# One VectorE operation per head for the joined rows of later node tiles, and tanh in place of Exp for their shares

## The chip, the cores and the metric

The kernel runs on one core of one Trainium2 chip. The metric is the time of one execution on the device in microseconds (us), the median of several runs; 1% of it, 40 us, is about what a measurement of this kernel can tell from no change.

## What is computed

A graph attention layer over 6250 nodes with 256 features (4 heads of 64) and 206250 directed edges, added to the input through a relu, and then 30 iterations of a small feed-forward step on every node, added as well:

```python
def _gat_forward(x, edge_index, W, att_src, att_dst, bias):
    h = (x @ W).reshape(n, HEADS, HID)
    a_src = jnp.einsum('nhf,hf->nh', h, att_src)
    a_dst = jnp.einsum('nhf,hf->nh', h, att_dst)
    # edges: the given ones and one from every node to itself
    e = jax.nn.leaky_relu(a_src[src] + a_dst[dst], NEG_SLOPE)
    m = jax.ops.segment_max(e, dst, num_segments=n)
    num = jnp.exp(e - m[dst])
    denom = jax.ops.segment_sum(num, dst, num_segments=n)
    alpha = num / denom[dst]
    out = jax.ops.segment_sum(alpha[:, :, None] * h[src], dst, num_segments=n)
    return jax.nn.relu(out.reshape(n, HEADS * HID) + bias)

def step(h, _):                       # 30 times
    h = h + 0.01 * jnp.tanh(h)
    h = h * jax.nn.sigmoid(h)
    h = _layernorm(h, ln_w, ln_b)
    h = jnp.einsum('bsc,dc->bsd', h, W) + b
    return (h, None)

x = x + gat(_layernorm(x))
x = x + scan(step, _layernorm(x), 30)
```

## The kernel before

The 6250 nodes lie in 49 tiles of 128 rows (`X[P, NT, C]`, node p*49+t). `attention` fills the first 2477 us: it walks the sorted edges in 124 steps and leaves in DRAM, for every node, one row of 264 numbers (`sums`): for each head 64 weighted feature sums and the sum of the weights, and behind them the four maxima the weights were taken against. The edge from a node to itself is left out there; the node's own row with its four exponents stands in `haug` and `eself`.

`scan_ffn` follows. It joins the two for every node and runs the 30 iterations. Joining takes, per tile and head: the gathered maximum and the own exponent (`nmax`), both less that maximum (`below`), their Exp on ScalarE (`share`, L1347), the denominator `den` from the gathered weight sum times one share plus the other share, and `part`, both shares over `den` (function `norms`). Then the gathered row `S` times `part[0]` plus the own row `own` times `part[1]`, a relu, and the sum with `X`.

The 49 tiles come in eight parts, `FT = [0, 4, 8, 14, 21, ...]`. The first three (`FRONT = 3`) are joined before the iterations start. The other five, seven tiles each, are joined while the iterations of earlier nodes run; `Plan` holds for each of these parts the pass at which each stage begins and the distance between its tiles. Part 3 takes a tile every 3 passes, parts 4 to 7 one every 11 passes, with 80 passes from one part to the next. The stages of a later tile before the change: `fetch` (GpSimd issues the indirect DMA that gathers the row into `S`), `scale` (VectorE writes `S` times `part[0]` into `Hs`, one TENSOR_TENSOR of 128x256, L1492), `own` (GpSimd multiplies the own rows in place, L1294), `add` (TensorE adds the two by products with the identity into the PSUM tile `ps_m`, L1652 and L1653), `both` (VectorE, relu and sum with X, reading `ps_m`, L1504), `spread` (statistics, L1507); behind the seventh tile come `mean`, `root` and, on ScalarE, `ready` (L1362), which writes the normalised rows into `Hs` and makes the tile's chunk available.

The iterations are 750 passes, each one iteration of one chunk of two tiles (25 chunks, the last with one tile), in an order that `passes` works out from the passes at which chunks become ready. A pass of chunk q is: tanh on ScalarE (`th`, L1409), the addition on GpSimd (`h1`, L1301), silu on ScalarE (`h2`, L1386), statistics and their aggregate on VectorE (L1568, L1577), the inverse root on GpSimd (L1308, for three passes at once from pass 54), the transposition, the product with W on TensorE (L1676), and on VectorE the scaling from PSUM with the bias (`affine`, L1586). The transposition is TensorE's (L1662, copied by ScalarE, L1392) for the first 54 passes and every third afterwards; the others go through DRAM: ScalarE splits the words (`hs`, L1398), one DMA stores them and a transposing DMA reads them back.

Each engine's program is written out pass by pass: a function `step` per engine says what it issues at pass n, with fixed offsets (VectorE's statistics are for pass n+3, its affine for n-2 from pass 54; TensorE's product for n-4), and `due` puts the stages of the later parts at the start of a step. ScalarE, GpSimd and VectorE take their instructions in that order, so a stage that waits holds all that is behind it.

## Time and profile before

| what | us |
|---|---|
| median of 3 runs | 4014.36 |
| lowest and highest | 4007.2, 4033.22 |
| the profiled execution | 4010.27 |
| its span in the trace | 4008.5 |
| busy: PE, DVE, ACT, POOL | 1551.2, 3057.0, 2421.6, 3000.3 |

PE is TensorE's products, PEld its weight loads (beside the products), DVE VectorE, ACT ScalarE, POOL GpSimd. Busy shares over the whole span say little here, as the attention part and the iterations have different limits; the argument goes by stretches. A timeline row gives the start, the duration, the engine, the line, the operation, its output and inputs and how many instructions it groups. Durations of neighbours overlap a little, so what an engine can do at most is read from start to start while it does not idle.

### The profile page before, as it was taken

The page shows a single profiled execution, that of the slowest core. Times are in us where ns is not written, and L with a number is a line of the kernel's source. Part 1 is how long each engine was busy: PE and PEld are TensorE (multiplying, and loading weights), DVE is VectorE, ACT ScalarE, POOL GpSimd, SP SyncE. Part 2 cuts the span into 40 slices and gives each one's busy share as a digit, 9 for nine tenths or more (in the row PEclk, how much of TensorE's full clock was granted, in tenths as well). Part 3 has the DMA queues.
Part 4 walks back from the last instruction along what each step waited for, and adds up shares of the span by engine and source line. Part 5 has one row for each costly group of instructions (what it writes and reads, how often), then busy time and mean ns, then how long its engine had stood idle before and what let it go on. Part 6 is the DMA issues. An engine that isn't in the chain of part 4 may idle for free.

```text
span 4008.5 us, 38964 instructions
## 1 busy us (share of the span) xinstructions
PE 1551.2 (39%) x7562; PEld 1329.0 (33%) x7562; DVE 3057.0 (76%) x7257; ACT 2421.6 (60%) x3681; POOL 3000.3 (75%) x2871
## 2 busy tenths in 40 slices
PE   3400000000000000000000001899999999999998
PEld 2300000000000000000000001788888888888887
DVE  7467585867768577685867766788988989888898
ACT  4334353534434344353534344689999999999997
POOL 7676676767676676766767672899999998889887
PEclk8755555555555555555555555999999999999999
DMA  7355565656555565565656563047777777777677
GB/s 201 113 177 193 182 207 181 213 174 214 195 190 201 169 223 178 190 209 168 225 164 218 189 198 126 23 117 179 189 185 185 181 177 177 173 177 175 177 183 193
DMA packets 649205, 720.45 MB, mean 180 GB/s; under 512 B 513249, under 2 KB 515458, under 8 KB 632948
## 3 DMA queue, kind: packets, MB, share of 16 engines
q1 hardware_dynamic: 563604, 486.62, 40.7%
q0 software_dynamic: 83824, 230.16, 20.0%
q10 hardware_dynamic: 1536, 1.18, 0.1%
q14 instruction: 178, 1.46, 0.1%
q8 instruction: 63, 1.03, 0.1%
HBM read 249.79 MB, written 352.38 MB: 150 GB/s over the span
## 4 chain that ended last, share of the span: by engine, by line
issue 25%; PE 20%; ACT 12%; DVE 12%; POOL 10%; DMA 9%; another core or an unknown queue 8%; SPq 2%; DVEq 0%; ACTq 0%; POOLq 0%
PE ps L1676 17%; ACT G L654 7%; POOL G L747 6%; DVE RS L983 5%; DMA turned<-hs 3%; DVE psum L964 3%; POOL h L1301 2%; PE ps L1662 2%; DMA h2T<-turned 2%; DMA sums<-G 2%; SPq L1231 1%; ACT hs L1398 1%; DMA G<-haug,idx 1%; ACT th L1409 1%
## 5 line engine op out<-in xcount | busy, mean ns | idle before, releaser
L747 POOL DMA_INDIRECT G<-haug,idx x1612 | 1526.6, 947 | 713.1 <-issue 481.8
L1676 PE MATMUL ps<-WT,h2T 128*128 128x256 f32 x5880 | 1338.8, 381 | 19.9 <-DMA h2T<-turned 18.8
L1676 PEld LDWEIGHTS ps<-WT,h2T 128*128 128x128 f32 x5880 | 1091.7, 191 | 175.8 <-DMA h2T<-turned 40.5
L983 DVE TENSOR_TENSOR_SCAN RS<-keep,psum 128x845 f32<-128x845 f32 x496 | 939.8, 1897 | 186.9 <-remote 109.9
L1301 POOL TENSOR_TENSOR h<-Hs,th 128x512 f32<-128x512 f32 (+1 forms) x750 | 937.8, 1262 | 129.9 <-ACT th L1409 124.6
L1068 PE MATMUL psum<-AD,ones 128*128 128x512 f32 x2 | 2.1, 1142 | 2284.9 <-DVE AD L1085 2284.9
L646 ACT ACTIVATE decay<-el,ZC 128x4 f32<-128x4 f32 x124 | 37.1, 299 | 1278.4 <-remote 568.0
L654 ACT ACTIVATE G<-RS 128x845 f32<-128x845 f32 x496 | 782.0, 1723 | 43.4 <-DVE RS L983 34.0
L1586 DVE SCALAR_TENSOR_TENSOR Hs<-ps,rs,b 128x256 f32<-128x256 f32 x1470 | 675.0, 459 | 145.3 <-PE ps L1676 132.6
L1068 PEld LDWEIGHTS psum<-AD,ones 128*128 128x128 f32 x2 | 0.5, 313 | 2285.2 <-DVE AD L1085 2285.2
L1568 DVE BATCH_NORM_STATS2 cst<-h 128x6 f32<-128x256 f32 x1470 | 546.3, 412 | 37.5 <-ACT h L1386 36.4
L964 DVE TENSOR_TENSOR psum<-G,psum 128x845 f32<-128x845 f32 x496 | 479.0, 1030 | 67.1 <-issue 62.9
L1386 ACT ACTIVATE h<-h 128x512 f32<-128x512 f32 (+1 forms) x750 | 459.4, 613 | 66.1 <-POOL h L1301 65.2
L1398 ACT ACTIVATE hs<-h 128x1024 uint16<-128x1024 uint16 x444 | 464.8, 1047 | 9.9 <-DMA turned<-hs 9.5
L1409 ACT ACTIVATE th<-Hs 128x512 f32<-128x512 f32 (+1 forms) x750 | 458.3, 611 | 7.5 <-DVE Hs L1586 6.7
L1308 POOL TENSOR_TENSOR rs<-cmv,half_neg 128x6 f32<-128x6 f32 (+1 forms) x286 | 353.1, 1235 | 14.7 <-DVE cmv L1577 13.7
L973 DVE SCALAR_TENSOR_TENSOR psum<-RS,decay,psum 128x65 f32<-128x65 f32 x492 | 125.3, 323 | 205.9 <-remote 205.6
L1662 PE MATMUL ps<-ident,h 128*128 128x128 f32 x1164 | 180.5, 277 | 24.5 <-ACT h L1386 18.1
L1577 DVE BATCH_NORM_AGGREGATE cmv<-cst 128x2 f32<-128x9 f32 x1470 | 188.1, 168 | 1.1
L1392 ACT ACTIVATE h2T<-ps 128x512 f32<-128x512 f32 (+1 forms) x306 | 171.4, 561 | 18.1 <-PE ps L1662 17.9
L1662 PEld LDWEIGHTS ps<-ident,h 128*128 128x128 f32 x1164 | 146.4, 142 | 61.7 <-ACT h L1386 26.0
L922 DVE TENSOR_TENSOR z<-G,AD 128x52 f32<-128x52 f32 x124 | 29.9, 241 | 165.8 <-DMA G<-haug,idx 132.3
(164 smaller groups left out, 1196.9 us busy)
## 6 DMA issues: line engine op xcount, KB each, us to landing
sums<-G SPq DMA_DIRECT2D x124, 1716.0 KB
turned<-hs SPq DMA_DIRECT2D x444, 256.0 KB
G<-haug,idx POOLq DMA_INDIRECT x1612
h2T<-turned SPq DMA_TRANSPOSE x444
haug<-G SPq DMA_DIRECT2D x7, 924.0 KB
X<-x SPq DMA_DIRECT2D x7, 784.0 KB
out<-X SPq DMA_DIRECT2D x24, 224.0 KB
own<-haug SPq DMA_DIRECT2D x5, 924.0 KB, 5.5
```

Of the source, the lines that this page charges most:

```text
L654: last = nc.scalar.activation(G[:, k % R, :, h * HR:(h + 1) * HR].rearrange("p t f -> p f t"), RS[:, k % 2, h, :, :], ACT.Copy)
L747: pool.indirect_dma_start(out=G[:, u, t, :], out_offset=None, in_=haug[:, :], in_offset=bass.IndirectOffsetOnAxis(ap=idx[:, i % 2, u * T + ...
L964: last = v.tensor_tensor(ps_m[:, h, :, :].rearrange("p f t -> p t f"), G[:, u, :, h * HR:(h + 1) * HR], w, ALU.mult)
L983: v.tensor_tensor_scan(RS[:, k % 2, h, :, :].rearrange("p f t -> p (f t)"), keep[:, k % 2, :, :].rearrange("p f t -> p (f t)"), ps_m[:, h, ...
L1301: g.tensor_tensor(h1[:, q.t, 0:n], chunk_rows(Hs, q.j, q.w), th[:, q.t, 0:n], ALU.add).then_inc(s_add, 1)
L1386: nc.scalar.activation(h2[:, q.u, 0:n], h1[:, q.t, 0:n], ACT.Silu, scale=1.0 / HS).then_inc(s_silu, 1)
L1398: nc.scalar.activation(hs[:, q.t, :].bitcast(U16).rearrange("p (l c) -> p l c", l=2), h2[:, q.u, :].bitcast(U16).rearrange("p (c l) -> p l ...
L1409: nc.scalar.activation(th[:, q.t, 0:n], chunk_rows(Hs, q.j, q.w), ACT.Tanh, scale=1.0 / HS).then_inc(s_tanh, 1)
L1568: last = v.bn_stats(cst[:, q.v, a, 0:6], h2[:, q.u, a * C:(a + 1) * C])
L1586: ins = v.scalar_tensor_tensor(out=Hs[:, q.j * CH + a, :], in0=ps_g[q.u][:, a * C:(a + 1) * C], scalar=rs[:, q.v, a:a + 1], in1=b100[:, :] ...
L1662: last = nc.tensor.transpose(ps_x[q.x][:, n * P:(n + 1) * P], h2[:, q.u, n * P:(n + 1) * P], ident[:, :])
L1676: last = nc.tensor.matmul(ps_g[q.u][:, a * C:(a + 1) * C], h2T[:, q.u, (a * 2 + k) * P:(a * 2 + k + 1) * P], WT[:, k, :], start=(k == 0), ...
```

## The change

For the later parts the gathered rows are no longer scaled into `Hs` ahead of time, and TensorE no longer adds. One VectorE operation per head (`joined`, 64 columns, four for a tile) takes `S` times `part[0]` plus the own rows, all in SBUF, into `Hs`, one step behind it the relu and the sum with `X` read `Hs` instead of PSUM. The two shares are written as 1 + tanh(d/2) and 1 - tanh(d/2) with d the difference of the two exponents, which have the same ratio as the two Exp; this holds for all eight parts. The maximum goes, an addition of 1.0 comes. Ahead of the first part a tanh of one column is issued on ScalarE. The plans lose a stage, and mean, root and ready come 4 passes earlier (3 for part 3), with which the order of the passes shifts in places. The semaphore of an own-row load is now one per buffer. The diff, cut where lines only rename:

```diff
-    def __init__(self, fetch, pace, below, share, norm, scale, own, add, both, step, mean, root, ready, every):
+    def __init__(self, fetch, pace, below, share, norm, own, join, both, step, mean, root, ready, every):
         n = QT
         self.at = dict(fetch=(fetch, pace, n), below=(below, 1, 1), share=(share, 1, 1), norm=(norm, 1, 1),
-                       scale=(scale, step, n), own=(own, step, n), add=(add, step, n), both=(both, step, n),
+                       own=(own, step, n), join=(join, step, n), both=(both, step, n),
...
-PLANS = {FRONT: Plan(5, 1, 10, 17, 15, 16, 22, 23, 21, 3, 43, 48, 50, 1)}
+PLANS = {FRONT: Plan(5, 1, 10, 17, 15, 20, 18, 19, 3, 40, 45, 47, 1)}
 for b in range(FRONT + 1, NF):
     q = 24 + 80 * (b - FRONT - 1)
-    PLANS[b] = Plan(q, 8, q + 54, q + 62, q + 63, q + 64, q + 70, q + 72, q + 72, 11, q + 141, q + 148, q + 151, 3)
+    PLANS[b] = Plan(q, 8, q + 54, q + 62, q + 63, q + 69, q + 67, q + 68, 11, q + 137, q + 144, q + 147, 3)
...
-        nmax = sb("nmax", [P, 2, QT, H])
-        below = sb("below", [P, 2, 2, QT, H])
+        apart = sb("apart", [P, 2, 2, QT, H])
         share = sb("share", [P, 2, 2, QT, H])
+        spare = sb("spare", [P, 1])
...
-            loads = {PLANS[b - 2].last("add") + 2: b for b in range(FRONT + 2, NF)}
+            loads = {PLANS[b - 2].last("own") + 2: b for b in range(FRONT + 2, NF)}
...
-                    pool.wait_ge(s_weighted, tiles_before(b - 1))
+                    pool.wait_ge(s_joined, tiles_before(b - 1))
...
-                nc.scalar.activation(share[:, b % 2, :, 0:n, :], below[:, b % 2, :, 0:n, :], ACT.Exp).then_inc(s_share, 1)
+                nc.scalar.activation(share[:, b % 2, :, 0:n, :], apart[:, b % 2, :, 0:n, :], ACT.Tanh, scale=0.5).then_inc(s_share, 1)
...
+            act.wait_ge(s_merged, 16)
+            nc.scalar.activation(spare[:, :], half_neg[:, 0:1], ACT.Tanh)
...
-                ch.add(v.tensor_tensor(nmax[:, i, 0:n, :], S[:, i, 0:n, SUMS:ROW], eself[:, t0:t1, :], ALU.max))
-                ch.wait()
-                v.tensor_tensor(below[:, i, 0, 0:n, :], S[:, i, 0:n, SUMS:ROW], nmax[:, i, 0:n, :], ALU.subtract)
-                v.tensor_tensor(below[:, i, 1, 0:n, :], eself[:, t0:t1, :], nmax[:, i, 0:n, :], ALU.subtract).then_inc(s_below, 1)
+                v.tensor_tensor(apart[:, i, 0, 0:n, :], S[:, i, 0:n, SUMS:ROW], eself[:, t0:t1, :], ALU.subtract)
+                v.tensor_tensor(apart[:, i, 1, 0:n, :], eself[:, t0:t1, :], S[:, i, 0:n, SUMS:ROW], ALU.subtract).then_inc(s_below, 1)
...
+                ch.add(v.tensor_scalar(share[:, i, :, 0:n, :], share[:, i, :, 0:n, :], 1.0, None, ALU.add))
+                ch.wait()
...
+            def joined(b, i):
+                for h in range(H):
+                    c = slice(h * HR, h * HR + HID)
+                    last = v.scalar_tensor_tensor(out=Hs[:, FT[b] + i, h * HID:(h + 1) * HID], in0=S[:, b % 2, i, c],
+                                                  scalar=part[:, b % 2, 0, i, h:h + 1], in1=own[:, b % 2, i, c],
+                                                  op0=ALU.mult, op1=ALU.add)
+                return last
...
-                if due(q, "scale"):
-                    b, i = due(q, "scale")
+                if due(q, "both"):
+                    b, i = due(q, "both")
+                    dve.wait_ge(s_joined, tiles_before(b) + i + 1)
+                    added(b, i, i + 1, Hs[:, FT[b] + i, :]).then_inc(s_taken, 1)
+                if due(q, "join"):
+                    b, i = due(q, "join")
                     if i == 0:
                         dve.wait_ge(s_part, b + 1)
-                    gathered(b, i, i + 1).then_inc(s_weighted, 1)
-                if due(q, "both"):
-                    b, i = due(q, "both")
-                    n = tiles_before(b) + i
-                    dve.wait_ge(s_joined, n + 1)
-                    added(b, i, i + 1, ps_m).then_inc(s_taken, 1)
+                    dve.wait_ge(s_ownt, tiles_before(b) + i + 1)
+                    joined(b, i).then_inc(s_joined, 1)
...
-            def add_tile(b, i):
-                n = tiles_before(b) + i
-                pe.wait_ge(s_weighted, n + 1)
-                pe.wait_ge(s_ownt, n + 1)
-                wait_count(pe, s_taken, n)
-                to = heads(ps_m, HID)
-                nc.tensor.matmul(to, ident[:, :], heads(Hs[:, FT[b] + i, :], HID), start=True, stop=False)
-                nc.tensor.matmul(to, ident[:, :], heads(own[:, b % 2, i, :], HR), start=False, stop=True).then_inc(s_joined, 1)
...
-                if due(p, "add"):
-                    add_tile(*due(p, "add"))
```

In the order of instructions of VectorE, at the third tile of part 3 (`S` the gathered rows, `partw` the shares over the denominator, `ps` PSUM, `X` the residual), before:

```order
L1586 SCALAR_TENSOR_TENSOR Hs<-ps,rs,b 128x256
L1568 BN_STATS cst<-h 128x6 x2
L1586 SCALAR_TENSOR_TENSOR Hs<-ps,rs,b 128x256
L1577 BN_AGGR cmv<-cst 128x2 x2
L1586 SCALAR_TENSOR_TENSOR Hs<-ps,rs,b 128x256
L1504 SCALAR_TENSOR_TENSOR X<-ps,X 128x256
L1568 BN_STATS cst<-h 128x6 x2
L1586 SCALAR_TENSOR_TENSOR Hs<-ps,rs,b 128x256
L1577 BN_AGGR cmv<-cst 128x2 x2
L1586 SCALAR_TENSOR_TENSOR Hs<-ps,rs,b 128x256
L1492 TENSOR_TENSOR Hs<-S,partw 128x256
L1507 BN_STATS bst<-X 128x6
```

and now:

```order
L1595 SCALAR_TENSOR_TENSOR Hs<-ps,rs,b 128x256
L1510 SCALAR_TENSOR_TENSOR Hs<-S,partw,own 128x64 x4
L1577 BN_STATS cst<-h 128x6 x2
L1595 SCALAR_TENSOR_TENSOR Hs<-ps,rs,b 128x256
L1586 BN_AGGR cmv<-cst 128x2 x2
L1595 SCALAR_TENSOR_TENSOR Hs<-ps,rs,b 128x256
L1504 SCALAR_TENSOR_TENSOR X<-Hs,X 128x256
L1577 BN_STATS cst<-h 128x6 x2
L1595 SCALAR_TENSOR_TENSOR Hs<-ps,rs,b 128x256
L1586 BN_AGGR cmv<-cst 128x2 x2
L1595 SCALAR_TENSOR_TENSOR Hs<-ps,rs,b 128x256
L1516 BN_STATS bst<-X 128x6
```

The one TENSOR_TENSOR of 256 columns became four operations of 64 columns with three inputs, and the addition reads `Hs` in SBUF where it read PSUM; the statistics of the tile stay one pass behind it.

TensorE at the first tile of part 3 (L1662 are transpositions, L1676 the products with W, `Hs` and `own` the two rows to be added), as a difference:

```order
 L1662 MATMUL ps<-ident,h 128x128 x4
 L1676 MATMUL ps<-WT,h2T 128x256 x4
-L1652 MATMUL ps<-Hs,ident 128x256
-L1653 MATMUL ps<-own,ident 128x256
 L1662 MATMUL ps<-ident,h 128x128 x4
 L1676 MATMUL ps<-WT,h2T 128x256 x4
```

Two additions of the tile are gone, and nothing comes in their place.

ScalarE at the share of part 4 (`share` the shares, `th` tanh, `h` silu, `hs` split words), before:

```order
L1386 ACTIVATE h<-h 128x512
L1409 ACTIVATE th<-Hs 128x512
L1386 ACTIVATE h<-h 128x512
L1347 ACT_TABLE_LOAD
L1347 ACTIVATE share<-below 128x56
L1409 ACTIVATE th<-Hs 128x512
L1398 ACTIVATE hs<-h 128x1024
L1386 ACT_TABLE_LOAD
L1386 ACTIVATE h<-h 128x512
```

and now:

```order
L1384 ACTIVATE h<-h 128x512
L1407 ACTIVATE th<-Hs 128x512
L1384 ACTIVATE h<-h 128x512
L1345 ACTIVATE share<-apart 128x56
L1407 ACTIVATE th<-Hs 128x512
L1396 ACTIVATE hs<-h 128x1024
L1384 ACTIVATE h<-h 128x512
```

Both table loads around the share are gone, and the other rows keep their order.

## Rows read from the trace of the kernel before

**Rows 1.** Busy by window: start:end, us, PE, PEld, DVE, ACT, POOL, clock, DMA, GB/s

```profile
2719.66:2880.03 160.37, 158.41 (x780) 136.99 (x779) 145.55 (x517) 152.28 (x246) 148.29 (x122) 1.00 0.79 190
...
3041.28:3203.00 161.72, 158.79 (x778) 136.52 (x777) 144.00 (x518) 154.01 (x250) 148.31 (x123) 1.00 0.76 181
3400.00:3800.00 400.00, 395.08 (x1966) 343.77 (x1965) 346.00 (x1244) 386.03 (x660) 358.97 (x293) 1.00 0.70 174
```

**Rows 2.** Timeline of TensorE, front part and without parts: start, us

```profile
2572.53 0.60 PE L1662 MATMUL ps<-ident,h 128*128 128x128 f32 x4
...
2574.69 0.59 PE L1652 MATMUL ps<-Hs,ident 128*128 128x256 f32 x2
...
2575.56 0.60 PE L1662 MATMUL ps<-ident,h 128*128 128x128 f32 x4
...
3373.18 0.60 PE L1662 MATMUL ps<-ident,h 128*128 128x128 f32 x4
...
3378.80 0.60 PE L1662 MATMUL ps<-ident,h 128*128 128x128 f32 x4
```

**Rows 3.** Lines of TensorE, 2480 to 4009: count, busy us, mean ns, idle before

```profile
L1652 PE MATMUL ps<-Hs,ident 128*128 128x256 f32 x70 | 20.8, 379 | 0.0
```

**Rows 4.** Timeline of VectorE, one pass

```profile
2903.69 0.74 DVE L1568 BATCH_NORM_STATS2 cst<-h 128x6 f32<-128x256 f32 x2
...
2904.91 0.43 DVE L1586 SCALAR_TENSOR_TENSOR Hs<-ps,rs,b 128x256 f32<-128x256 f32 x1
2905.26 0.74 DVE L1568 BATCH_NORM_STATS2 cst<-h 128x6 f32<-128x256 f32 x2
```

**Rows 5.** Lines of VectorE, 2700 to 3400, and the last from 2480 to 4009

```profile
L1492 DVE TENSOR_TENSOR Hs<-S,partw 128x256 f32<-128x256 f32 x28 | 23.8, 851 | 0.0
L1507 DVE BATCH_NORM_STATS2 bst<-X 128x6 f32<-128x256 f32 x28 | 11.7, 416 | 0.0
L1504 DVE SCALAR_TENSOR_TENSOR X<-ps,X 128x256 f32<-128x256 f32 x28 | 11.6, 413 | 0.0
L1469 DVE TENSOR_TENSOR nmax<-S,eself 128x28 f32<-128x28 f32 x4 | 3.4, 848 | 0.0
...
L1516 DVE TENSOR_SCALAR ve<-mv 128x7 f32<-128x7 f32 x4 | 0.6, 161 | 0.0
...
L1504 DVE SCALAR_TENSOR_TENSOR X<-ps,X 128x1024 f32<-128x1024 f32 x2 | 2.4, 1224 | 2.6 <-PE ps L1643 2.5
```

**Rows 6.** Timeline of ScalarE, three passes and a table load

```profile
2709.56 0.58 ACT L1392 ACTIVATE h2T<-ps 128x512 f32<-128x512 f32 x1
...
2715.05 0.58 ACT L1392 ACTIVATE h2T<-ps 128x512 f32<-128x512 f32 x1
...
2864.98 1.28 ACT L1347 ACT_TABLE_LOAD   x1
2866.27 0.25 ACT L1347 ACTIVATE share<-below 128x56 f32<-128x56 f32 x1
```

**Rows 7.** Timeline of VectorE and GpSimd at a gathered product

```profile
2946.53 2.52 POOL L1301 TENSOR_TENSOR h<-Hs,th 128x512 f32<-128x512 f32 x2 [0.63 <-ACT th L1409]
...
2947.99 1.35 DVE L1492 TENSOR_TENSOR Hs<-S,partw 128x256 f32<-128x256 f32 x1
```

**Rows 8.** Timeline of VectorE at the subtractions of two parts

```profile
2552.63 1.98 DVE L1472 TENSOR_TENSOR below<-eself,nmax 128x28 f32<-128x28 f32 x1
...
2859.92 1.20 DVE L1471 TENSOR_TENSOR below<-S,nmax 128x28 f32<-128x28 f32 x1
...
2861.05 0.17 DVE L1472 TENSOR_TENSOR below<-eself,nmax 128x28 f32<-128x28 f32 x1
```

**Rows 9.** Lines of GpSimd, 2700 to 3350

```profile
L1301 POOL TENSOR_TENSOR h<-Hs,th 128x512 f32<-128x512 f32 x326 | 414.4, 1282 | 50.4 <-ACT th L1409 46.5 <-DVE Hs L1586 0.3 <-issue 0.2
```

**Rows 10.** Waits between 2700 and 3350: us in total, times, longest

```profile
POOL h L1301 <- ACT th L1409: 46.5, 76, 2.1
```

More of the change, by code:

```diff
@@ L1168, in scan_ffn @@
         ps_x = [psum[:, n * 512:(n + 1) * 512] for n in (4, 5)]
-        ps_m = psum[:, 6 * 512:6 * 512 + C]
-        s_own = [sem(f"s_own{b}") for b in range(NF)]
+        s_own = [sem(f"s_own{n}") for n in range(2)]
         s_S = [sem(f"s_S{q}") for q in range(FLY)]
@@ L1176, in scan_ffn @@
         s_ownt = sem("s_ownt")
-        s_weighted = sem("s_weighted")
         s_joined = sem("s_joined")
@@ L1220, in own_rows @@
                 t0, t1 = FT[b:b + 2]
-                sp.dma_start(own[:, b % 2, 0:t1 - t0, :], haug.rearrange("(p i) c -> p i c", i=NT)[:, t0:t1, :]).then_inc(s_own[b], 16)
+                sp.dma_start(own[:, b % 2, 0:t1 - t0, :], haug.rearrange("(p i) c -> p i c", i=NT)[:, t0:t1, :]).then_inc(s_own[b % 2], 16)
             def send(q):
@@ L1290, in own_tile @@
                 if i == 0:
-                    pool.wait_ge(s_own[b], 16)
+                    pool.wait_ge(s_own[b % 2], 16 * (b // 2 + 1))
                     pool.wait_ge(s_part, b + 1)
@@ L1346, in shares @@
                 n = FT[b + 1] - FT[b]
-                nc.scalar.activation(share[:, b % 2, :, 0:n, :], below[:, b % 2, :, 0:n, :], ACT.Exp).then_inc(s_share, 1)
+                nc.scalar.activation(share[:, b % 2, :, 0:n, :], apart[:, b % 2, :, 0:n, :], ACT.Tanh, scale=0.5).then_inc(s_share, 1)
             def own_tile(b, i):
                 if i == 0:
-                    act.wait_ge(s_own[b], 16)
+                    act.wait_ge(s_own[b % 2], 16 * (b // 2 + 1))
                     act.wait_ge(s_part, b + 1)
@@ L1532, in all_weighted @@
                 ch.add(gathered(b, 0, n))
-                dve.wait_ge(s_own[b], 16)
+                dve.wait_ge(s_own[b % 2], 16 * (b // 2 + 1))
                 own_rows(b, OWN_ACT[b], n).then_inc(s_scaled, 1)
```

## The prediction

> **What bounds the kernel now.** I read the busy shares by stage first. The attention, up to 2477 us, is not touched by the change. In the passes of the feed-forward scan that have later parts among them TensorE is busy for 158 to 159 of every 161 us, ScalarE for 154, GpSimd for 148 and VectorE for 145, at full granted clock [rows 1]: no engine has much room, and TensorE has the least. Three such windows follow each other, from 2719.66 to 3203.00, each 80 passes and one later part of seven tiles (they run from one part's norms to the next); the first and the last stand there, and their mean is 483.34 / 3 = 161.1.
>
> Next the timeline of TensorE gives its price per pass. In a stretch without later parts three passes (two with a DMA turn, one turned by TensorE) run from 3373.18 to 3378.80, 5.62 us, or 1.873 a pass [rows 2]. Eighty take 149.9 us. In the front part a pass is 2.16 us (2572.53 to 2574.69), and the products that add a tile's own rows fill 2574.69 to 2575.56, 0.87 us with no gap [rows 2]. The lines view counts 70 products on the first of the two lines that add a tile, two a tile for 35 tiles, and the second has as many [rows 3]. So an 80-pass cycle needs 149.9 + 7 x 0.87 = 156.0 us of TensorE and lasts 161.1: 5.1 us are lost to waits. The window without parts (3400 to 3800) has 1966 TensorE instructions; at 9.33 a pass that is 210.6 passes, 394.5 us of need in 400: there only 1.4% is lost.
>
> Then the others by the same method, start to start while they do not idle. VectorE: one pass is 2903.69 to 2905.26, 1.57 us [rows 4], 80 are 125.6. A tile adds the gathered product (0.851 mean), the addition from PSUM (0.413) and one statistics operation (0.416), less 0.08 each by which successors overlap (the operation of 0.43 us at 2904.91 is followed after 0.35), 1.44 us, seven make 10.1; the small operations of a part sum to 15.3 us for four parts in that answer (ten groups, nmax the first, ve the last), 3.8 each [rows 5]. VectorE needs 139.5. ScalarE: three passes run from 2709.56 to 2715.05, 5.49 us, 146.4 for 80; seven normalisations, put at 0.5 each, and one share add 3.8, and the two table loads 2.6 and a little lost overlap, 2.8: 153.0 [rows 6]. GpSimd by its busy time: 148.4.
>
> **The change part by part.** *Products of TensorE.* 35 x 0.87 = 30.4 us leave TensorE; its need falls to 149.9 a cycle. *Exp to tanh.* Each of five parts loses two loads of 1.28 us [rows 6]; the order of instructions keeps a single one, ahead of the first silu. ScalarE falls to 150.2. The extra activation at the start is one column and sits where ScalarE waits for gathered rows anyway: nothing. *Shares and norms.* One maximum with its wait goes, one addition of 1.0 with its wait comes, both on 28 to 56 elements: nothing, bounded by 0.5 us either way per part. *Steps.* Mean, root and ready come four passes earlier; all 750 passes are still to be done and none was starved, so nothing. The later own-row load is asked for three passes earlier and has tens of passes of room. The join now waits for GpSimd's own tile: that is issued right behind GpSimd's addition of pass 93, which VectorE's statistics of the same pass, one step ahead of the join, already need, so no wait, or at most the length of that one operation.
>
> *VectorE per tile, the term that decides.* Out go the product (0.851) and the addition from PSUM. In come four operations of 64 columns and an addition from SBUF. None of the two forms is in this stretch. Their own length I take from the same instruction at two sizes: 412 ns at 256 and 1224 at 1024 columns is 1.06 ns a column [rows 5], so 64 columns are 0.21 long and 0.15 apart (0.35 less 192 x 1.06 ns): four 0.60, the addition 0.35. Without waits that is 0.95 against 1.11 before (1.26 less the overlap), a gain of 0.16.
>
> But they wait. The gathered product at 2947.99 took 1.35 us, against 0.41 for the addition of the same size from PSUM, and ended 0.3 us behind the second of the two GpSimd additions of 2.52 us [rows 7]. The addition from PSUM shows none of this, mean 0.413 [rows 5]. So an operation with two SBUF inputs waits while GpSimd adds (mean 0.44: 0.851 less 0.41), and one that reads PSUM does not. The Trainium skill (SBUF — State Buffer, "Who interferes with whom") has this as a rule against such a change: a VectorE instruction with two SBUF inputs and a GpSimd instruction that reads SBUF exclude each other for the whole instruction, and whichever issues first goes. The trace agrees for one instruction. By the rule each of the five new ones could meet a GpSimd addition of its own.
>
> What four in a row do is bounded by the pairs of small subtractions: at 2552.63 the second of a pair lost its turn to the next GpSimd addition and took 1.98 us, though the first had just waited; at 2859.92 only the first waited, 1.20, and the second passed in 0.17 [rows 8]. The second lost in one of five such pairs. I take this row count: three followers with a chance of 0.2 each at 1.28 us (GpSimd's addition [rows 9]) cost 0.77. Tile: 0.95 + 2 x 0.44 + 0.77 = 2.60, against 1.11, +1.5 us. Bounds: -0.16 (no wait), and +6.2 (all five wait out 1.28: 0.95 + 6.4 = 7.35). VectorE's cycle need becomes 139.5 + 10.5 = 150.0. GpSimd is held back in turn, at most by the 0.6 us more a tile that VectorE's operations of this form now run (0.95 against 0.35): 148.4 + 4 = 152.
>
> *Sum.* Before, one engine at 156.0 led, the next at 153.0, and 5.1 us were lost. After, the four stand at 152, 150.2, 150.0 and 149.9. Four level engines that feed one another lose more; I take 6, so 158 a cycle, 3.1 less. Four cycles (28 tiles) give 12 us. In the front part three passes and a tile take 3 x 2.16 + 0.87 = 7.35 us on TensorE before; after, TensorE would need 6.5 but VectorE 3 x 1.57 + 2.6 + 0.33 = 7.6, so those seven tiles give 0 (bounds -6 and +2). The profiled execution took 4010.3 us (span 4008.5); 4010.3 - 12 = 3998. It stands 4 us under the median of the three runs, 4014.4, so I put the median at 4000.
>
> **The rivals.** *All of TensorE's time is given back.* For it: it led by 3 us, and without parts the loss was 1.4%. Then a cycle is 149.9 x 1.014 = 152.0, 9.1 less, 36 for four, and 6 in the front: 3968. Against it: GpSimd's 148.4 and ScalarE's 150.2 leave no room for that smoothness. *Nothing is given back*, because GpSimd and ScalarE set the pace: GpSimd waits for tanh 46.5 us between 2700 and 3350 [rows 10], in a loop that does not contain TensorE's additions. Then a cycle stays near 161: 4010 to 4014. *The joins lose their turns.* After each 64-column operation GpSimd's waiting addition goes first. It decides from the point where VectorE's need passes 156, that is 16.5 / 7 = 2.4 us more a tile, a tile at 3.5, or (3.5 - 1.83) / 1.28 = 1.3 lost turns. With two lost turns a tile is 4.4, the cycle need 162.5 and the cycle 167.4: +6.3, 25 for four, and in the front 4.7 + 4.4 + 0.3 = 9.4 against 7.4, +14 for seven tiles: 4010 + 39, about 4050. With every turn lost: need 183, cycle 185, +96, and +35 in the front: 4140. Against it: GpSimd can only run ahead by the few passes its buffers allow and then idles, and four of five pairs kept the turn. *The tables stay.* The order of instructions shows them gone, so this has no chance of its own.
>
> **How the numbers follow.** My forecast, 3990 to 4008: 0.55. All given back, 3960 to 3985: 0.10. Nothing given back: 0.20. Turns lost, from 4018 up: 0.15, half of it under 4050. A measurement of this kernel can tell about 1% from no change, 40 us: faster than 3974 is only the best part of the second case, 0.04; slower than 4054 the worse half of the last, 0.07; within 1%, 0.89. The range leaves out the best of the second case and the worst of the last: 3980 to 4032, the upper end being some 1.7 lost turns.
>
> **What would show it.** Right: TensorE has no lines for later own rows and waits more for turned rows than before; a cycle of 80 passes of 157 to 159 us; the four joined operations of a tile together about 1.8 us with most of the wait on the first; the addition from SBUF at 0.8 mean; five fewer pairs of table loads. Wrong: joined operations that each take over 1 us, or a cycle still at 161 with VectorE under 90% busy, or one of 152.

## The result and the profile after

| | median us | lowest to highest | runs |
|---|---|---|---|
| before | 4012.31 | 4000.28 to 4033.22 | 17 |
| changed | 4028.4 | 4007.7 to 4057.68 | 17 |

The ratio of the changed kernel to the kernel before is 1.0043, with a 95% interval of 1.0025 to 1.006: some 17 us slower, where 12 us faster were forecast. The median lies within the stated range of 3980 to 4032, but above the kernel before and not below it, in the part from 4018 up that the prediction gave 0.15.

Busy time by window in the changed kernel, the columns as in [rows 1] (PE, PEld, DVE, ACT, POOL, clock, DMA, GB/s); the first three windows are again 80 passes each, from norms to norms:

```profile
2720.45:2885.20 164.75, 156.06 (x748) 131.71 (x747) 156.94 (x539) 149.01 (x243) 149.21 (x124) 0.99 0.76 184
2885.20:3049.43 164.23, 155.56 (x748) 131.41 (x746) 154.06 (x538) 151.01 (x246) 146.79 (x122) 0.99 0.77 180
3049.43:3213.24 163.81, 156.04 (x753) 130.77 (x752) 157.23 (x539) 152.50 (x250) 148.64 (x124) 1.00 0.77 179
3400.00:3800.00 400.00, 397.55 (x1980) 345.69 (x1979) 347.88 (x1251) 387.02 (x663) 359.80 (x295) 1.00 0.70 174
```

Against [rows 1] a cycle has grown from 161.1 to 164.3 us, while TensorE's program has 28 instructions fewer in it and, from 3400 on, goes at least as fast as before. VectorE is now busy for 156 of 164 us, where it was busy for 145 of 161. TensorE still shows 156 busy us where 80 passes need 150 by the prediction's count, so its busy column does not show the room that it has. GpSimd, which the prediction put at up to 152, stays at 148.2 on the mean of the three (148.3 in the first and last of [rows 1]): in these windows only VectorE got fuller. The two profiled executions split like this (from the start of `den`, L1478, of one part to that of the next, and to the span's end):

| stretch | before | changed |
|---|---|---|
| scan up to the norms of part 3 | 81.4 | 79.2 |
| norms of part 3 to norms of part 4 | 156.4 | 159.5 |
| three cycles | 483.5 | 492.8 |
| norms of part 7 to the end | 805.7 | 809.3 |

Lines of the changed kernel between 2700 and 3400 (VectorE) and 2480 to 4023 (TensorE), columns as in [rows 5] and [rows 3]:

```profile
L1510 DVE SCALAR_TENSOR_TENSOR Hs<-S,partw,own 128x64 f32<-128x64 f32 x112 | 66.3, 650 | 0.0
L1504 DVE SCALAR_TENSOR_TENSOR X<-Hs,X 128x256 f32<-128x256 f32 x28 | 21.1, 752 | 0.0
```

```profile
L1676 PE MATMUL ps<-WT,h2T 128*128 128x256 f32 x5880 | 1348.5, 383 | 37.6 <-DMA h2T<-turned 36.0 <-ACT h2T L1390 0.3
```

A joined operation of 64 columns takes 650 ns on the mean and the addition from SBUF 752, where the addition from PSUM took 413 [rows 5]. TensorE's idle time ahead of the products with W is 37.6 us in the scan, 36.0 of it for chunks that the DMA turns. On the page of the kernel before the same group stood at half of that, over its whole span:

```profile
L1676 PE MATMUL ps<-WT,h2T 128*128 128x256 f32 x5880 | 1338.8, 381 | 19.9 <-DMA h2T<-turned 18.8
```

What a joined tile can take is seen at its shortest and near its longest. First VectorE at 2861, then VectorE and GpSimd from 2575:

```profile
2861.47 0.86 DVE L1510 SCALAR_TENSOR_TENSOR Hs<-S,partw,own 128x64 f32<-128x64 f32 x4
2862.25 0.75 DVE L1577 BATCH_NORM_STATS2 cst<-h 128x6 f32<-128x256 f32 x2
```

```profile
2575.01 4.83 DVE L1510 SCALAR_TENSOR_TENSOR Hs<-S,partw,own 128x64 f32<-128x64 f32 x4
...
2577.85 1.98 DVE L1510 SCALAR_TENSOR_TENSOR Hs<-S,partw,own 128x64 f32<-128x64 f32 x1
...
2579.75 0.74 DVE L1577 BATCH_NORM_STATS2 cst<-h 128x6 f32<-128x256 f32 x2
```

```profile
2574.03 1.28 POOL L1299 TENSOR_TENSOR h<-Hs,th 128x512 f32<-128x512 f32 x1
2575.26 0.70 POOL L1306 TENSOR_TENSOR rs<-cmv,half_neg 128x2 f32<-128x2 f32 x1
2575.94 1.26 POOL L1299 TENSOR_TENSOR h<-Hs,th 128x512 f32<-128x512 f32 x1
2577.17 0.67 POOL L1292 TENSOR_TENSOR own<-own,partw 128x256 f32<-128x256 f32 x1
2577.81 0.69 POOL L1306 TENSOR_TENSOR rs<-cmv,half_neg 128x2 f32<-128x2 f32 x1
2578.49 1.26 POOL L1299 TENSOR_TENSOR h<-Hs,th 128x512 f32<-128x512 f32 x1
```

Four joined operations that meet nobody take 0.86 us. In the other tile they take 4.83 (the second row is the fourth of them by itself). It is issued at 2577.85, when GpSimd has just begun its inverse root, does not get in between that and the addition at 2578.49, and ends at 2579.83, right behind the addition: a lost turn as in [rows 8]. Over the 35 tiles the sum of four runs from 0.86 to 4.91 us with a mean of 2.44, so 1.58 us of a tile are waits.

How a stop of VectorE reaches the others is seen in the group of GpSimd that reads VectorE's aggregates, between 2700 and 3350 us (columns as in [rows 9]), before and after:

```profile
L1308 POOL TENSOR_TENSOR rs<-cmv,half_neg 128x6 f32<-128x6 f32 x108 | 146.3, 1355 | 2.4 <-DVE cmv L1577 2.1
```

```profile
L1306 POOL TENSOR_TENSOR rs<-cmv,half_neg 128x6 f32<-128x6 f32 x107 | 143.3, 1339 | 22.4 <-DVE cmv L1586 22.3
```

GpSimd's inverse root waited 2.1 us for VectorE's aggregates before the change and waits 22.3 us now. VectorE's scaling of the product needs that root, and GpSimd's next additions stand behind it.

The tables did what was forecast: around the share of part 7 no load stands.

```profile
3199.05 0.63 ACT L1384 ACTIVATE h<-h 128x512 f32<-128x512 f32 x1 [1.01 <-POOL h L1299]
3199.59 0.23 ACT L1345 ACTIVATE share<-apart 128x56 f32<-128x56 f32 x1
3199.73 0.61 ACT L1407 ACTIVATE th<-Hs 128x512 f32<-128x512 f32 x1
```

### The profile page after: what moved, and what is told of

Its sections match the earlier page's. It is cut to its first block, busy times and chain, and to the rows that moved or that the text cites. A ratio compares the mean times of both kernels' runs of the same rounds, so it can differ in the third digit from the quotient of the medians.

```text
span 4022.5 us, 38750 instructions
## 1 busy us (share of the span) xinstructions
PE 1538.4 (38%) x7422; PEld 1303.5 (32%) x7422; DVE 3110.8 (77%) x7362; ACT 2406.7 (60%) x3672; POOL 2995.3 (74%) x2871
## 4 chain that ended last, share of the span: by engine, by line
issue 21%; DVE 16%; ACT 14%; PE 13%; another core or an unknown queue 12%; POOL 10%; DMA 9%; SPq 3%; DVEq 0%; ACTq 0%; POOLq 0%
PE ps L1676 10%; ACT G L654 8%; POOL G L747 6%; DVE RS L983 5%; DMA turned<-hs 4%; DVE psum L964 3%; POOL h L1299 3%; DMA h2T<-turned 2%; SPq L1229 2%; DVE cst L1577 2%; DMA G<-haug,idx 2%; DMA sums<-G 2%; ACT hs L1396 1%; DVE Hs L1595 1%
## 5 line engine op out<-in xcount | busy, mean ns | idle before, releaser
L1676 PE MATMUL ps<-WT,h2T 128*128 128x256 f32 x5880 | 1348.5, 383 | 37.6 <-DMA h2T<-turned 36.0
L1676 PEld LDWEIGHTS ps<-WT,h2T 128*128 128x128 f32 x5880 | 1094.1, 191 | 203.2 <-DMA h2T<-turned 66.7
L1662 PE MATMUL ps<-ident,h 128*128 128x128 f32 x1164 | 182.6, 279 | 33.7 <-ACT h L1384 21.2
L1662 PEld LDWEIGHTS ps<-ident,h 128*128 128x128 f32 x1164 | 145.5, 143 | 76.6 <-ACT h L1384 41.6
```

The source lines that it names most:

```text
L1676: last = nc.tensor.matmul(ps_g[q.u][:, a * C:(a + 1) * C], h2T[:, q.u, (a * 2 + k) * P:(a * 2 + k + 1) * P], WT[:, k, :], start=(k == 0), ...
```

## The experiments

Each session timed some kernels together with the kernel before. Sessions differ: in some the attention stage runs about 260 us faster (the scan began at 2481 us in the trace before, and at about 2221 in those). The chip does not decide it alone, as the record has one chip number in sessions of both kinds (5: tanh_split_load and tanh_split_again, one program with cycles of 158.7 and 160.3 us). So kernels are compared by their ratio to the kernel before in the same session, and cycles between traces by length. "Cycle" below is the mean of the three 80-pass cycles in the one profiled execution of a kernel; single cycles of one execution differ by 1 to 9 us. A mean is good to about 2 by our estimate; the two programs traced twice differ by 0.6 (the change) and 1.6 us (tanh with split loads).

| kernel | ratio to before | 95% interval | cycle us | norms 3 to 4 us |
|---|---|---|---|---|
| the change, first result | 1.0043 | 1.0025 to 1.006 | 164.3 | 159.5 |
| change_again | 1.0036 | 1.0017 to 1.0055 | 164.9 | 160.6 |
| late_ready | 1.0019 | 1.001 to 1.0028 | 164.4 | 159.8 |
| join_only | 1.0068 | 1.0054 to 1.0081 | 167.0 | 161.9 |
| join_psum_in | 0.9989 | 0.998 to 0.9998 | 161.5 | 152.0 |
| join_out_psum | 1.0022 | 1.0006 to 1.0037 | 162.7 | 159.3 |
| head_a_pass | 1.0035 | 1.0024 to 1.0046 | 165.9 | 160.0 |
| tanh_only | 0.9984 | 0.9975 to 0.9993 | 160.5 | 154.7 |
| double_products | 1.0028 | 1.0018 to 1.0039 | 164.4 | 160.4 |
| no_products | 0.9973 | 0.9952 to 0.9995 | 160.3 | 151.5 |
| no_gathered | 0.9953 | 0.994 to 0.9967 | 160.7 | 150.5 |
| no_own | 0.9943 | 0.9929 to 0.9956 | 159.8 | 148.5 |
| no_load | 0.9927 | 0.9903 to 0.9952 | 156.6 | 148.6 |
| no_fetch | 0.9891 | 0.987 to 0.9912 | 152.8 | 148.7 |
| join_in_psum | 0.9981 | 0.9958 to 1.0003 | 160.6 | 151.7 |
| psum_split_load | 0.9981 | 0.9972 to 0.999 | 160.4 | 152.8 |
| tanh_split_load | 0.9975 | 0.9958 to 0.9992 | 158.7 | 154.4 |
| tanh_split_again | 0.9981 | 0.9972 to 0.9991 | 160.3 | 154.4 |
| change_split_load | 1.0019 | 1.0002 to 1.0036 | 163.0 | 160.0 |

### Where the loss is: the join's second SBUF input

join_psum_in leaves the own rows out of the sum: the second input is whatever stands in PSUM.

```diff
-    scalar=part[:, b % 2, 0, i, h:h + 1], in1=own[:, b % 2, i, c],
+    scalar=part[:, b % 2, 0, i, h:h + 1], in1=ps_m[:, h * HID:(h + 1) * HID],
```

> The changed kernel, with the second input of the four joined operations read from PSUM instead of the own rows in SBUF (the own rows are left out of the sum; GpSimd still scales them). Theory 1, turns: the joined operations lose turns to GpSimd's additions because both their inputs are in SBUF; then each tile's four take 0.8 to 0.9 us together instead of the mean 2.44, none over 1.1, an 80-pass cycle falls from 164.3 to 156-159 us and the kernel to 0.993-0.997 of the kernel before. Theory 2, plan: the slowdown comes from the shifted stages and order of passes; then the time stays at 1.004. Theory 3, level engines: TensorE's time was never wanted, and VectorE's waits are hidden; then 1.000, or 1.004 if the join's own length costs.

Measured 0.9989. The line view of its joined operations (duration min/median/max in ns):

```profile
L1511 DVE SCALAR_TENSOR_TENSOR Hs<-S,partw,ps x140: 261/272/276, 2309.0 to 3073.4; 128x64 f32<-128x64 f32 x140
```

and the same view of the changed kernel:

```profile
L1510 DVE SCALAR_TENSOR_TENSOR Hs<-S,partw,own x140: 270/277/3298, 2567.8 to 3349.3; 128x64 f32<-128x64 f32 x140
```

Same operation, same count, same place and same columns: with one input in PSUM none of 140 waits, with both in SBUF the longest waits 3.0 us. The Trainium skill (SBUF — State Buffer, "Who interferes with whom") states that a VectorE instruction with two SBUF inputs contends with a GpSimd instruction that reads SBUF, and that one with at most one SBUF input, outside the 2-port modes, does not. The trace agrees: 140 of 140 with one such input pass in 276 ns or less. Taking that wait away gives back 0.5% (1.0043 to 0.9989, 20 us), the whole loss, as theory 1 has it for the cause; GpSimd's wait for the aggregates falls back to 6.9 us in as long a stretch. But what theory 1 forecast beyond that, 0.993 to 0.997 and cycles of 156 to 159 us, did not come. The kernel is level with tanh_only (0.9984, same session), its cycle is 161.5, and on this half theory 3 was right. The 0.5% goes across sessions. Within one session there are late_ready, 10 us above join_psum_in, and join_in_psum below, 15 us under change_again with the whole computation in place. Where TensorE's time went is the second question.

late_ready has the old passes for mean, root and ready (for part 3 too: 43, 48 and 50):

```diff
-    ... q + 68, 11, q + 137, q + 144, q + 147, 3)
+    ... q + 68, 11, q + 141, q + 148, q + 151, 3)
```

> The changed kernel with mean, root and ready of every part back at the passes of the kernel before, so the order of the 750 passes is the old one. Theory 1 (turns): 1.003 to 1.006 of the kernel before, cycles still 163 to 165 us. Theory 2 (plan and order of passes): back to 1.000, cycles 161.

1.0019 lies between the two expectations, above no change; its cycle, 164.4, is the changed kernel's. So the old order of passes does not bring the time back, and theory 2 is at most a part. Whether the shifted stages cost a tenth or two of a per cent is open: change_again, in another session, has 1.0036, and the intervals overlap.

> The changed kernel unaltered, as the standard for the runs beside it, since the chip of the experiments runs the attention stage some 265 us faster than the first one and the scan the same. All theories: 1.0045 of the kernel before, 17 us; if the plan has a part in it, this stands clearly above late_ready's 1.0019.

Its session turned out to be one with the longer attention stage (4005.82 us for the kernel before), and 1.0036 does not stand clearly above late_ready.

join_only is the changed kernel with Exp, the maximum and no addition of 1.0.

> The changed kernel with the shares by Exp of the difference to the maximum again, so only the join is new. Theory 1 (turns): the join alone costs more than the whole change, 1.005 to 1.008 of the kernel before. If tanh brings nothing: 1.004 as the whole change.

1.0068, as expected. What the tables gave hid a part of what the join costs.

join_out_psum writes the join to PSUM and the addition reads it there.

> The changed kernel with only the output of the four joined operations moved to PSUM, so their inputs stay in SBUF and the addition behind them reads PSUM. Theory 1 (turns): the four keep their mean of 0.66 each, the addition falls from 0.68 to 0.41 us, and the kernel lies 2 to 5 us under change_again. If writing to SBUF were part of the wait: the four fall to 0.3 each and the kernel to 0.998.

The joined operations keep 645 ns, the addition falls to 410, and the median lies 1.6 us under change_again's (5.6 us by the ratios; the intervals overlap). The output is not what waits. With the input's test above, the two SBUF inputs are.

head_a_pass spreads the four over four passes, one each. Its edit does more than its expectation says: the addition and the statistics come three passes later, and mean, root and ready of parts 4 to 7 stand at the old passes, as in late_ready.

> The changed kernel with the four joined operations of a tile of parts 4 to 7 in four passes, one each, instead of in one (part 3 as changed). The work is the same. Theory 1, where a burst of lost turns of up to 4.9 us holds the affine of VectorE and so the loop: no single stop over 2 us, 5 to 10 us under change_again, 1.001 to 1.0025. If only the sum of the waits counts: four waits of 0.44 make 1.8 as before, 1.0035.

1.0035, with a mean of 759 ns for an operation against 653 in change_again. Spreading them gains nothing, so the forecast gain of 5 to 10 us did not come. Four operations now take 3.0 us instead of 2.6 in sum, as each meets GpSimd on its own, so a gain from shorter stops may be hidden under longer waits: this run speaks for the sum of the waits but does not rule out the bursts.

### What TensorE's time is worth

tanh_only is the kernel before with the new shares.

> The kernel before with only the shares by tanh. Ten table loads go, 13 us of ScalarE. Theory 1 (turns): this part of the change is a gain, 0.997 to 0.9995 of the kernel before, as ScalarE was the second engine and its bursts of 2.8 us held TensorE; cycles 159 to 161 us. Theory 3 (ScalarE or GpSimd set the pace): if it is ScalarE the whole 13 us appear, 0.997; if GpSimd, 1.000.

0.9984, 6 us of the 13 that ScalarE saves. no_products leaves TensorE's additions out of it (VectorE and the loads of own rows wait for GpSimd's own tile instead):

```diff
-    dve.wait_ge(s_joined, n + 1)
+    dve.wait_ge(s_ownt, n + 1)
...
-                if due(p, "add"):
-                    add_tile(*due(p, "add"))
```

> The kernel before with the shares by tanh (tanh_only, 0.9984), and the products with which TensorE adds the later tiles left out: VectorE's addition reads PSUM as it is, after GpSimd's own tile. It measures what TensorE's 30 us are worth by themselves. As predicted (TensorE leads and the rest follows): 25 to 35 us under tanh_only, 0.990 to 0.992, cycles 152 to 155 us. Theory 3 (GpSimd, ScalarE and the loop of a chunk are as full as TensorE): at most 10 us under tanh_only, 0.996 to 0.998, cycles 158 to 160 with TensorE idle in its place.

0.9973 where 0.990 to 0.992 were forecast if TensorE led. Against tanh_only that is 4 us, not told apart from nothing; at their ends the two intervals leave at most 16 us, about half of the forecast. In the traces the gain is all in the stretch of part 3, 154.7 to 151.5 us; the cycles stand at 160.5 and 160.3. A window of 480 us over its three cycles:

```profile
2720.00:3200.00 480.00, 463.09 (x2240) 394.31 (x2239) 435.60 (x1545) 450.83 (x735) 443.79 (x368) 0.99 0.75 186
```

2240 instructions are exactly 240 passes in 480 us, 160.0 for 80, with 449.5 us of need (240 x 1.873). double_products issues them twice.

> tanh_only with the two products of each later tile issued twice, so TensorE has 30 us more. If TensorE leads a cycle, as the prediction had it: 25 to 35 us over tanh_only, 1.005 to 1.007 of the kernel before, cycles 166-167 us. If it is one of several with 10 us to spare in a cycle of 160: 3 to 12 us over tanh_only, 0.999 to 1.002, nearly all of it in part 3.

1.0028: 16 us over tanh_only (0.0044) for 30 us more work. That lies between the two expectations, and it is not nearly all in part 3. TensorE's need in a cycle is then 162.1 and the cycle is 164.4. So three points are known: need 149.9 gives 160.3, 156.0 gives 160.5, 162.1 gives 164.4. There is a floor at about 160 that TensorE does not set. With the loss of 1.4% that the stretch without parts showed, a need of 162.1 makes 164.4, the measured cycle, and 156.0 makes 158.2, under the floor. By this estimate the knee lies at a need of about 158, and the kernel before stood just below it: two us more a cycle would have cost, and six less bought nothing.

### What holds the floor

From no_products on, one piece after another was left out, the earlier ones staying out (the sums of the later tiles are left incomplete): VectorE's scaling of the gathered rows, GpSimd's scaling of the own rows, the three later loads of own rows, and the gathers of parts 5 to 7 (the diff has one line of each, in this order: no_gathered, no_own, no_load, no_fetch; waits that hung on a piece are moved or left out with it).

```diff
-                    gathered(b, i, i + 1).then_inc(s_weighted, 1)
...
-                    own_tile(*due(p, "own"))
...
-                    own_rows(b)
...
-                if due(p, "fetch"):
+                if due(p, "fetch") and due(p, "fetch")[0] < FRONT + 2:
```

> no_products with VectorE's scaling of the gathered rows left out as well (the later tiles' sums are wrong in both). VectorE has 0.9 us a tile less and no operation with two SBUF inputs in a tile. If the waits of VectorE at GpSimd's additions set the cycle of 160 us: cycles 155 to 157, 15 to 25 us under no_products, 0.991 to 0.994. If the cycle is a matter of GpSimd and ScalarE or of the loop of a chunk: at most 8 us, 0.995 to 0.998, cycles 158 to 160.

> no_gathered with GpSimd's scaling of the own rows left out too, so a later tile costs only its fetch, one addition from PSUM, one statistics and one normalisation. If GpSimd is what is full beside TensorE: another 10 to 20 us, cycles 152 to 154, 0.989 to 0.992. If the loop of a chunk holds the cycle (ten passes apart): under 5 us more and cycles still at 157 to 160 with every engine under 93% busy.

> no_own with the three later loads of own rows (924 KB each, in the midst of the chunks' turns) left out as well; nothing reads them there. If a load's traffic, which held a turn for 3 to 7 us in each of the traces so far, is what keeps the cycle at 160: 8 to 15 us under no_own, 0.990 to 0.992, two of the three cycles at 155 or less. If not: under 4 us.

> no_load with the gathers of parts 5 to 7 left out too (21 software DMAs and 1.04 us of GpSimd each). If the gathers' traffic or GpSimd's time keeps the cycle: 15 us or more under no_load, cycles 152 to 154. If the passes themselves, with ten chunks that follow each other at a distance of ten, take 2.0 us: cycles stay at 157 to 160 with next to no work of the later tiles left.

Neither VectorE's nor GpSimd's scaling moves the cycle: 160.7 and 159.8. What they give is small and in part 3. With the loads gone it is 156.6, with the gathers gone as well 152.8. no_load falls short of what was forecast for the load alone (6 us by the ratios instead of 8 to 15, one cycle under 155 instead of two); no_fetch does what was forecast. What a load can do is seen in no_own: SyncE's queue, then ScalarE.

```profile
2591.99 0.33 SPq L1218 DMA_DIRECT2D own<-haug  x1
2592.41 2.66 SPq L1228 DMA_TRANSPOSE h2T<-turned  x1
2595.20 0.98 SPq L1223 DMA_DIRECT2D turned<-hs  x2
2600.01 2.57 SPq L1228 DMA_TRANSPOSE h2T<-turned  x2
```

```profile
2600.08 1.06 ACT L1394 ACTIVATE hs<-h 128x1024 uint16<-128x1024 uint16 x1 [4.26 <-DMA turned<-hs]
```

The load of 924 KB is issued at 2592.0. Between 2596.2 and 2600.0 the queue issues no turn, since the store of the chunk ahead of it has not landed (the queue's own wait for it is 3.8 us); ScalarE waits 4.26 us for a store to free a buffer. Slow stores are not the load's alone: the same trace has stores that take over 4 us where no load runs (4.9 at 2533.3, against a median of 2.5). Without the load and the gathers TensorE's and VectorE's waits shrink and ScalarE fills (no_fetch, 480 us):

```profile
2715.00:3195.00 480.00, 474.31 (x2339) 411.29 (x2338) 437.40 (x1595) 470.00 (x773) 427.15 (x340) 1.00 0.78 184
```

ScalarE is busy for 470 of 480 us and TensorE runs 2339 instructions, 250.6 passes, 153 us for 80, near its need of 150. So the floor of 160 goes when loads and gathers are both gone (0.9943 to 0.9891, intervals apart). That it is their traffic, which delays the turned chunks, is the likely reading and not shown. How much is the load's and how much the gathers' is not separated by the ratios: no_own and no_load overlap (other sessions), no_load and no_fetch, in one session, are 18 us apart in the median with intervals that just overlap; and no_fetch also frees GpSimd of 21 issues of 1.04 us, so traffic and GpSimd's time are not told apart there. For the load, the runs with split loads below find nothing to gain from taking its burst away.

### Versions that compute everything

join_in_psum keeps the join on VectorE without any operation of two SBUF inputs: TensorE lays the scaled own rows into PSUM with one product a tile, the join reads and writes that tile, the addition reads it. The join comes one pass (part 3) or two passes (parts 4 to 7) later for it.

```diff
+                nc.tensor.matmul(heads(ps_m, HID), ident[:, :], heads(own[:, b % 2, i, :], HR), start=True, stop=True)
...
-    out=Hs[:, FT[b] + i, h * HID:(h + 1) * HID], ... in1=own[:, b % 2, i, c],
+    out=ps_m[:, h * HID:(h + 1) * HID], ... in1=ps_m[:, h * HID:(h + 1) * HID],
```

> The changed kernel with one product a tile on TensorE that lays the scaled own rows into PSUM; the four joined operations read the gathered rows from SBUF and that tile, write back to PSUM, and the addition reads PSUM. None of the five has two SBUF inputs. Theory 1 (turns): the five take their own length, 0.85 and 0.41 us, and the kernel comes out under tanh_only: 0.994 to 0.998. Theory 3: level with tanh_only, 0.998 to 0.999. Theory 2 (plan): 1.001 or more.

0.9981, and 284 ns for a joined operation. In the same session change_again took 1.0036, and the intervals do not meet: with the computation whole, the waits of two SBUF inputs are again the loss. It is level with tanh_only, as theory 3 has it, but its interval also holds the upper part of what theory 1 forecast. The loads by single tiles, one every 11 passes, for parts 6 and 7:

```diff
-                    own_rows(b)
+                        own_row(b, i)
```

> tanh_only with the own rows of parts 6 and 7 loaded tile by tile, one every 11 passes, instead of 924 KB at once. The whole computation stands. If the load's burst holds the turns: 3 to 8 us under tanh_only, 0.9965 to 0.998 of the kernel before, and no wait for a turned chunk over 3 us. If not: as tanh_only, 0.998 to 0.999.

> The changed kernel with the own rows of parts 6 and 7 loaded tile by tile. If the changed kernel's loss were a collision of the load with a burst of the join: back to 1.000 to 1.002. If the lost turns at GpSimd are a loss of their own: 1.002 to 1.004, 3 to 8 us under change_again.

> join_in_psum with the own rows of parts 6 and 7 loaded tile by tile; the whole computation stands. No operation of a tile has two SBUF inputs, TensorE has half the additions, ScalarE no table loads, and the load's burst is gone. If TensorE's time counts once the bursts are gone: 3 to 10 us under tanh_split_again, 0.995 to 0.997 of the kernel before. If it still does not: level with it, 0.997 to 0.998.

> tanh_split_load unaltered, to stand beside psum_split_load on the same chip and to narrow its ratio: 0.997 to 0.998.

0.9975 and 0.9981 for tanh with split loads against 0.9984 for tanh alone: not told apart. The changed kernel with split loads is still slower than the kernel before (1.0019, where both theories met; its median is 16 us over tanh_split_load's in the same session), so its loss is not, or not in the main, a collision with the load. psum_split_load and tanh_split_again are equal, 3742.99 and 3742.43 us: the half of TensorE's additions that the first leaves out buys nothing there either. tanh_only and its split form beat the kernel before by 0.16% to 0.25% and the change by 0.5% to 0.7%.

## Why the prediction was wrong

*The attention and the front.* Untouched, as said.

*Exp to tanh.* Right: ten loads gone, tanh_only gains 6 us, and join_only against the change shows 0.25%, across sessions.

*TensorE's products.* The step "one engine at 156.0 led, ... 5.1 us were lost" took the leader's need plus a loss for the mechanism of the cycle, and let the released 6.1 us a cycle count. This step failed. no_products measures the release alone: 4 us in the kernel (not told apart from 0) where 30 us of work went, and 0.2 us in a cycle of 160. TensorE was indeed the engine nearest its limit and, with two more products a tile, it does set the time; but its waits for turned chunks were read as a loss on top of its need, not as another bound under it. In the changed kernel they doubled (18.8 to 36.0 us ahead of the products): 17 us of the 30 that were freed went there. The rival "Nothing is given back" was right on this half, though not for its reason: neither GpSimd's scaling nor VectorE's moved the cycle; the loads and gathers of the later tiles, left out together, did.

*VectorE per tile.* The mechanism was right, the size too small. Forecast were 0.60 for four joined operations without waits, 0.44 for each of two first waits and 0.77 for lost turns, together 2.60. Measured in the cycles: 66.3 / 28 = 2.37 for the four and 0.75 for the addition, less 0.16 of overlap, 2.96. The four are 0.86 long on their own; two in a row start about 0.2 apart, not 0.15, so the slope between 256 and 1024 columns does not hold down to 64. The waits of the four are 1.51 in the cycles instead of 1.21: the first of a tile waits 0.62 (0.89 less its length of 0.27) where 0.44 was taken, the three behind it 0.90 where 0.77 was. Of 105 followers in the 35 tiles 29 took over 1 us, 0.28 where the five pairs gave 0.2. The addition came out shorter, 0.59 without the overlap where 0.79 was taken. GpSimd was not held back. The tile stayed under the 3.5 us that the rival of the lost turns named as its point, and the kernel was slower all the same, because that point was worked out from a TensorE need of 156 that did not hold the cycle.

*The sum.* The loss of 6 us on top of the fullest engine was chosen and not worked out, and it is the term that missed most; with VectorE at 139.5 + 7 x 1.85 = 152.5 the cycle is 164.3, a loss of 12. Some 8 of these 12 lie under the floor of about 160, which was there before (160.5 in tanh_only). The rest, 4 us, comes with the stops: VectorE's aggregates and affine sit in the loop of every chunk, GpSimd's wait for the aggregates rose from 2.1 to 22.3 us, and with the joined inputs freed of waits the cycle falls to 161.5. How the stops add up with what holds the floor is not shown; no run takes this loop apart further.

*The front part.* Forecast 0 us, bounds -6 and +2. From norms 3 to norms 4 it is 3.1 us longer than before, and 4.8 longer than tanh_only in the same stretch; no_products puts TensorE's part there at -3.2. It is the one stretch in which both halves of the argument hold.

*Steps.* The shift of mean, root and ready was put at nothing; late_ready leaves up to 0.2% open.

*The signs.* Of those named for being right, three came: TensorE waits more for turned rows, the addition from SBUF takes about 0.8, and the table loads are gone. Two did not: the cycle is 164.3 instead of 157 to 159, and the four take 2.4 instead of 1.8, with less than half of the wait on the first.

## What to carry to other kernels

Ask of a fused operation first where its inputs lie. Here each with both inputs in SBUF stopped when it met a GpSimd instruction that reads SBUF, and four small ones waited 1.5 us a tile where one large one had waited 0.44. One input in PSUM took the wait away. An engine that is busiest is not thereby the one whose work pays: leave the work out in a trial, double it in another, and the two points together say what a microsecond there is worth and on which side of a floor the kernel stands. When all engines stand between 90 and 99% and the time does not follow any of them, leave out the DMAs of the work in question too, one kind at a time.

## What the runs showed of the hardware

- A 64-column operation with three inputs takes 0.27 us each, some 0.20 apart, 0.86 us for four in a row, with the rows of both inputs in SBUF and nobody in the way, and 0.26 to 0.28 for each of 140 with one of them in PSUM.
- A VectorE operation that waits for GpSimd can be passed over at the end of one GpSimd instruction and go only behind the next (the 1.98 us at 2577.85; the longest of 140 took 3.3 us, more than two additions of 1.28). GpSimd's additions did not get longer by it: 1282 ns on the mean before, 1279 after.
- Spread over four passes, the operations take longer each (759 ns) than in one row (653 ns).
- The same program takes some 260 us less in some sessions (3745 against 4005 us in all), and the difference lies in the attention stage (scan from 2221 instead of 2481 us). One chip number has both (3749.9 and 4004.7 us for the kernel before).
